# The ranking phase of a routed expert layer: statistics by chunk, tile products on ScalarE, reordered last steps, and logits with the gate stationary

## The chip, the cores and the metric

The kernel runs on one core of a Trainium2 chip. The metric is the device time of one execution in microseconds, as the median of several runs. The program computes a two-layer transformer with two expert layers; the change is in one phase near its end.

## What is computed

```python
x = x + attention(layernorm(x));  x = x + latent_moe(layernorm(x))
x = x + linear_attention(layernorm(x))
x = x + capacity_moe(layernorm(x))          # 4096 tokens of 256
# capacity_moe, up to the experts:
logits = x @ gate_weight.T                  # 128 experts, 48 of them kept
logits = where(old_to_new == -1, -inf, logits)
top_v, top_i = top_k(softmax(logits), 8)
top_v = top_v / sum(top_v)
oh = one_hot(old_to_new[top_i].reshape(-1)) # 4096*8 choices x 48 experts
pos = sum(cumsum(oh) * oh) - 1              # place of a choice in its expert's list
valid = pos < 96                            # an expert takes its first 96 tokens
# then each kept expert gathers its tokens, computes, and adds its weighted result back
```

## The kernel before, in words

Five engines run their own instruction lists, written out by hand, and wait for each other through semaphores. `ranking_phase` works on the 4096 tokens in 8 chunks of 512, each of four tiles of 128 tokens. It is a software pipeline of 13 steps: in step `i`, `now(i, back)` names chunk `i - back`, so different parts of the lists work on different chunks.

For a chunk, in order: VectorE finishes the residual sum of each tile (its first product, of `acc`, `rs` and `x`), takes its mean and variance (`variances`); ScalarE takes roots, VectorE `scales`, and ScalarE writes the normalized `lines`. TensorE transposes the lines into `tr` in PSUM. ScalarE copies them into a high part `XH` of reduced mantissa, VectorE subtracts that for the low part `XL`, and TensorE makes the logits `LG` from three products of high and low parts with the gate's `GH` and `GL`, with a penalty row `pen` for experts that are not kept. VectorE finds the top eight (`top`), the largest negated (`ntop`), and who was chosen (`left`, `sel`); ScalarE takes the exponentials `ex`. GpSimd sums choices (`tally`, `before`) and masks the exponentials (`es`). TensorE counts the places (`POS`), VectorE keeps those of the chosen (`u`), and GpSimd splits each into an eighth `hi` and a rest `lo` (`t2`, `hi`, `lo`). VectorE compares: `A` over `hi`, and `B`, eight compares over `lo`. Then B is multiplied by the token's number within its tile (`BB[0:8]`, the place products, ScalarE) and by the tile's first token (`BB[8:16]`, the tile products, GpSimd), and TensorE adds the products of A and BB into the slots `SL`. GpSimd also makes the weights `w`, which SP's queue stores to memory beside the lines.

The statistics are taken in four runs of two chunks (`RUNS`, `RT`, `RC`): run 0 and run 1 ahead of the loop, run 2 in step 1 and run 3 in step 3. Behind step 12, VectorE and TensorE turn the slots into the list `idx`. Then `kept_experts_phase` begins behind a barrier.

Of the kernel before, what the change touches and what calls it, by code (L numbers as in the profile page):

```python
# [25 lines left out]
P = 128  # L26
# [2110 lines left out]
def ranking_phase(nc, raw, o2n, x_rows, x_first, acc, rs, ident, rows, out, idx):  # L2137
# [12 lines left out]
    with Phase(nc, "rank") as ph:  # L2150
# [17 lines left out]
        absent = ph.sb("absent", [1, KEPT])  # L2168
        pen = ph.sb("pen", [1, 1, KEPT])
# [4 lines left out]
        tile_i = ph.sb("tile_i", [P, TILES, KEPT], I32)  # L2174
        tile_no = ph.sb("tile_no", [P, TILES, KEPT], BF16)
# [31 lines left out]
        POS = ph.ps("POS", [P, CHUNK])  # L2207
        SL = ph.ps("SL", [CAP, 2, CHUNK])
# [6 lines left out]
        (pe_lg, dve_top, dve_left, dve_ntop, dve_sel, act_ex, pool_es, dve_total, dve_share, pool_w, pool_tally,  # L2215
         pool_before, pe_pos, dve_u, pool_round, pool_hi, pool_lo, dve_a, dve_b, act_bp, pool_bt, pe_slots) = ph.sems(
            "pe_lg dve_top dve_left dve_ntop dve_sel act_ex pool_es dve_total dve_share pool_w pool_tally "
            "pool_before pe_pos dve_u pool_round pool_hi pool_lo dve_a dve_b act_bp pool_bt pe_slots")
# [3 lines left out]
        STEPS = CHUNKS + 5  # L2222

# [37 lines left out]
        def _(pool):  # L2261
# [3 lines left out]
            nc.gpsimd.iota(tile_i[:], [[P, TILES], [0, KEPT]], base=0, channel_multiplier=0).then_inc(iotas, 1)  # L2265
# [11 lines left out]
            for i in range(STEPS):  # L2277
                g = now(i, 2)
                if g is not None:

                    pool.wait_ge(dve_sel, g + 1)
                    nc.gpsimd.tensor_tensor(tally[:, 0], sel[:, g % 2, 0, :], sel[:, g % 2, 1, :], ALU.add)\
                        .then_inc(pool_tally, 1)
                    nc.gpsimd.tensor_tensor(tally[:, 1], sel[:, g % 2, 2, :], sel[:, g % 2, 3, :], ALU.add)\
                        .then_inc(pool_tally, 1)
                    pool.wait_ge(act_ex, g + 1)
                    if g >= 3:
                        pool.wait_ge(dve_total, g - 2)
                    nc.gpsimd.tensor_tensor(es[:, g % 3], ex[:, g % 2], sel[:, g % 2], ALU.mult).then_inc(pool_es, 1)
                    pool.wait_ge(pool_tally, 3 * g + 2)  # L2290
                    nc.gpsimd.tensor_tensor(tally[:, 2], tally[:, 0], tally[:, 1], ALU.add).then_inc(pool_tally, 1)
                    pool.wait_ge(pool_tally, 3 * g + 3)
                    if g >= 1:
                        pool.wait_ge(pool_before, g)
                        pool.wait_ge(pe_pos, g)
                    nc.gpsimd.tensor_tensor(before[:, (g + 1) % 2], before[:, g % 2], tally[:, 2], ALU.add)\
                        .then_inc(pool_before, 1)

                g = now(i, 4)
                if g is not None:  # L2300
                    pool.wait_ge(dve_share, g + 1)
                    nc.gpsimd.tensor_tensor(w[:, tiles_of(g), :], es[:, g % 3],
                                            total[:, g % 2].to_broadcast([P, TPC, KEPT]), ALU.mult).then_inc(pool_w, 1)
                    pool.wait_ge(dve_b, g + 1)
                    if g >= 3:
                        pool.wait_ge(pe_slots, g - 2)
# [4 lines left out]
                g = now(i, 2)  # L2311
# [14 lines left out]

        @block.tensor
        def _(pe):
# [7 lines left out]
            nc.tensor.matmul(tr[:, 1, KD * KEPT:(KD + 1) * KEPT], ones[:], perm[:], start=True, stop=True)\  # L2336
                .then_inc(pe_gp, 1)
            pe.wait_ge(gates_ready, 1)
            pe.wait_ge(pen_ready, 1)
            pe.wait_ge(slots_set, 1)  # L2340
            for i in range(STEPS):
# [11 lines left out]
                if g is not None:  # L2353

                    pe.wait_ge(low_ready, g + 1)
                    if g >= 2:
                        pe.wait_ge(dve_left, g - 1)
                        pe.wait_ge(act_ex, g - 1)
                    b = g % 2
# [45 lines left out]
        def _(act):  # L2405
# [23 lines left out]
            for i in range(STEPS):  # L2429
                if i + 1 < CHUNKS:  # L2430
                    make_lines(i + 1)
# [407 lines left out]
```

## Time and profile before

| | |
|---|---|
| median of 3 runs | 2995.62 us (2993.15 to 3000.16) |
| the profiled execution | 2990.76 us, its span 2988.4 us |
| ranking phase in the span | 2656.8 to 2798.2 us |
| expert phase behind it | 2799.1 to 2988.4 us |
| mean granted TensorE clock, whole span | 0.933 |
| busy share of the whole span | PE 91%, DVE 56%, ACT 47%, POOL 27% |

The names in the profile: PE is TensorE, PEld its weight loads, DVE VectorE, ACT ScalarE, POOL GpSimd and SP the engine whose queue issues the transfers here. Tiles of the phase have the prefix `rank_`. An instruction's row gives its start, its duration, its line, what it writes and reads, and in brackets the idle time of its engine ahead of it with what ended that. The shares are of the whole program, and the phase is a twentieth of it, so they tell nothing of the phase.

### The profile page before, as it was taken

Reading aid. Unit: us, or ns where it says so; the run is one execution under the profiler, and the core shown is the slowest. Engines: PE = TensorE matmul, PEld = TensorE weight load, DVE = VectorE, ACT = ScalarE, POOL = GpSimd, SP = SyncE. Lnnn points to the kernel's source line nnn. Section 1 sums busy time; section 2 is a strip of 40 time slices with the busy share of each in tenths; the row PEclk is TensorE's granted clock in tenths of the full one; section 3 lists DMA queues with packets and bytes.
Section 4 is the critical chain, followed back from the end, with each engine's and each line's share of the span. In section 5 each row is a group of like instructions: output and inputs, shape, how many; then the busy total and the mean of one; then the engine's idle time right before and its main releaser. Section 6 shows DMA issues by size and latency. Waiting matters only on the chain. (4 is left out here: it accounts for less than half of the span.)

```text
span 2988.4 us, 50873 instructions
## 1 busy us (share of the span) xinstructions
PE 2734.3 (91%) x17834; PEld 2218.9 (74%) x17834; DVE 1686.7 (56%) x3254; ACT 1394.1 (47%) x2564; POOL 815.0 (27%) x817
## 2 busy tenths in 40 slices
PE   7899999989799998699999999999999999978573
PEld 6444444368578887598998989899898999967452
DVE  7688888446588887544444444444444444456321
ACT  6477777756478876433333333333333333324110
POOL 3522121200152221122222222222222222215675
PEclk9799999989899999799999999999999999975665
DMA  8955464030254553200000000000000000022476
GB/s 254 202 94 80 67 87 60 3 97 4 97 203 179 188 182 131 81 1 8 16 1 22 1 23 1 1 22 1 22 1 22 1 1 19 1 85 78 104 171 123
DMA packets 158642, 204.15 MB, mean 68 GB/s; under 512 B 17568, under 2 KB 134976, under 8 KB 149696
## 3 DMA queue, kind: packets, MB, share of 16 engines
q1 hardware_dynamic: 149904, 186.14, 23.5%
q0 software_dynamic: 8544, 15.22, 3.0%
q8 instruction: 146, 2.39, 0.3%
q14 instruction: 48, 0.39, 0.0%
HBM read 154.74 MB, written 50.78 MB: 69 GB/s over the span
## 5 line engine op out<-in xcount | busy, mean ns | idle before, releaser
L1846 POOL TENSOR_TENSOR lin_o2sum<-lin_o2sum,lin_o 128x512 f32<-128x512 f32 x128 | 183.8, 1436 | 1020.7 <-ACT lin_o L1883 1020.7
L875 DVE TENSOR_REDUCE score_pm<-score_SM 128x1 f32<-128x512 f32 (+3 forms) x608 | 364.5, 656 | 80.6 <-PE score_SM L735 47.7
L829 ACT ACTIVATE score_PR<-score_SE 128x512 f32<-128x512 f32 (+1 forms) x640 | 309.8, 557 | 106.3 <-PE score_SE L763 102.7
L2101 DVE TENSOR_TENSOR C_acc<-lin_OUT,C_acc 128x512 f32<-128x512 f32 x256 | 177.2, 692 | 266.3 <-PE lin_OUT L1963 264.7
L2084 DVE SCALAR_TENSOR_TENSOR lin_go<-lin_gT,lin_O 128x512 f32<-128x512 f32 x128 | 88.1, 688 | 421.0 <-PE lin_O L1999 377.2
L1866 ACT ACTIVATE lin_qT<-lin_PJ 128x512 f32<-128x512 f32 x129 | 77.0, 597 | 434.3 <-PE lin_PJ L1925 434.3
L1925 PE MATMUL lin_PJ<-C_XH,lin_WH 128*128 128x512 f32 x774 | 254.4, 410 | 14.0 <-DVE lin_WL L2040 14.0
L1925 PE MATMUL lin_PJ<-C_XL,lin_WH 128*128 128x512 f32 x774 | 241.3, 393 | 0.0
L1925 PE MATMUL lin_PJ<-C_XH,lin_WL 128*128 128x512 f32 x774 | 241.1, 393 | 0.0
L735 PE MATMUL score_SM<-A_KR,A_QR 96*128 96x512 bf16 (+3 forms) x768 | 229.9, 341 | 12.1 <-DVEq L81 9.4
L763 PE MATMUL score_SE<-A_QR,A_KR 99*128 99x512 bf16 (+3 forms) x768 | 210.7, 330 | 2.0 <-ACT score_PR L829 1.5
L1888 ACT ACTIVATE lin_goh<-lin_go 128x512 fp32r<-128x512 f32 x128 | 81.0, 633 | 260.2 <-DVE lin_go L2084 260.2
L1636 ACT ACTIVATE experts_h<-experts_z 128x512 f32<-128x512 f32 x256 | 161.1, 629 | 70.5 <-DVE experts_z L1541 67.0
L1996 PE MATMUL lin_O<-lin_sd,lin_v 128*128 128x128 f32 x1024 | 190.4, 275 | 3.1 <-issue 3.1
L1541 DVE SCALAR_TENSOR_TENSOR experts_z<-experts_HP,experts_sq 128x512 f32<-128x512 f32 x256 | 174.0, 686 | 17.7 <-PE experts_HP L1673 14.3
L1841 POOL TENSOR_TENSOR lin_qd<-lin_qT,lin_dec 128x512 f32<-128x512 f32 x128 | 166.0, 1297 | 47.0 <-DVE lin_dec L2066 36.1
L1999 PE MATMUL lin_O<-lin_qd,lin_kv 128*128 128x128 f32 x896 | 173.5, 275 | 0.0
L1996 PEld LDWEIGHTS lin_O<-lin_sd,lin_v 128*128 128x128 f32 x1024 | 160.2, 191 | 14.3 <-issue 4.8
L702 POOL TENSOR_SCALAR_AFFINE_SELECT score_PR<-score_PR 128x512 f32<-128x512 f32 x128 | 79.7, 634 | 333.7 <-ACT score_PR L829 333.7
L1925 PEld LDWEIGHTS lin_PJ<-C_XL,lin_WH 128*128 128x128 f32 x774 | 145.9, 189 | 33.1
L1925 PEld LDWEIGHTS lin_PJ<-C_XH,lin_WL 128*128 128x128 f32 x774 | 145.7, 188 | 32.6
L1548 DVE TENSOR_TENSOR experts_hl<-experts_h,experts_hh 128x512 fp32r<-128x512 f32 x192 | 139.7, 727 | 33.0 <-ACT experts_hh L1637 24.4
(357 smaller groups left out, 6715.3 us busy)
## 6 DMA issues: line engine op xcount, KB each, us to landing
experts_sq<-B_roots SPq DMA_DIRECT2D x64, 1024.0 KB, 4.7
A_QR<-q_parts SPq DMA_DIRECT2D x96, 128.0 KB, 6.4
A_KR<-k_parts SPq DMA_DIRECT2D x96, 128.0 KB, 6.9
kept_GU<-L_ffn_gate_up_proj SPq DMA_DIRECT2D x48, 192.0 KB, 2.8
v_rows<-inp_vt SPq DMA_DIRECT2D x32, 256.0 KB, 4.0
A_V<-v_rows SPq DMA_DIRECT2D x16, 512.0 KB, 10.8
C_w<-L_attn_w_qkv SPq DMA_DIRECT2D x27, 256.0 KB, 3.6
q_parts<-inp_parts SPq DMA_DIRECT2D x16, 384.0 KB, 3.6
```

Of the source, the lines that this page charges most:

```text
L735: ins = nc.tensor.matmul(SM[:, count % RING, at:at + nk], QR[0:ROWS_QK, u, h0 + j, t * P:(t + 1) * P], KR[0:ROWS_QK, u, h0 + j, k0:k0 + nk ...
L763: ins = nc.tensor.matmul(SE[:, e % RING, at:at + nq], KR[0:ROWS_ALL, u, h, kt * P:(kt + 1) * P], QR[0:ROWS_ALL, u, h, q:q + nq], start=Tru ...
L829: nc.scalar.activation(PR[:, st % BUFS, h, 0:width], SE[:, e % RING, 0:width], ACT.Exp, scale=SCALE)\
L875: nc.vector.tensor_reduce(pm[:, n % 2, h0:h0 + nh, t, k0 // CHUNK], SM[:, count % RING, 0:nh * nk].rearrange("p (h k) -> p h k", h=nh), AX ...
L1541: nc.vector.scalar_tensor_tensor(z[:, e % 2], HP[:, e % BUFS], 0.0, sq[:, (e // QE) % BUFS, e % QE], ALU.max, ALU.mult).then_inc(dve_z, 1)
L1636: nc.scalar.activation(h[:, e % BUFS], z[:, e % 2], ACT.Square).then_inc(act_h, 1)
L1841: nc.gpsimd.tensor_tensor(qd[:], qT[:, j], dec[:, j, 0:1, :].to_broadcast([P, B4, BLK]), ALU.mult).then_inc(pool_qd, 1)
L1846: nc.gpsimd.tensor_tensor(o2sum[:, c], o2sum[:, c], o2[:], ALU.add).then_inc(pool_sum, 1)
L1925: ins = nc.tensor.matmul(PJ[:, bank], a[:, w, k, j * DH:(j + 1) * DH], x[:, k, :, c, :], start=(n == 0), stop=(n == 3 * KD - 1))
L1996: ins = nc.tensor.matmul(O[:, b, :], v[:, c % 2, b, j * DH:(j + 1) * DH], sd[:, b, :], start=True, stop=(c == 0))
L1999: ins = nc.tensor.matmul(O[:, b, :], kv[:, j, b, :], qd[:, b, :], start=False, stop=True)
L2101: nc.vector.tensor_tensor(dst, OUT[:, half], dst, ALU.add).then_inc(dve_acc[half], 1)
```

## The change

It has four parts.

1. *Statistics by chunk.* `variances(run)` over eight tiles becomes `statistics(g)` over four. Ahead of the loop stand chunk 0 and, behind the constants, chunk 1. The others stand at the ends of steps 0 to 4, as `STATS_AT` says. Roots and scales are taken for the ranges of chunks in `VARY`. ScalarE's lines of the next chunk now stand behind the high part and the new copy.
2. *Tile products on ScalarE.* GpSimd's product over 1536 columns becomes four ScalarE copies with a constant scale, one for each tile, over 8x48 columns. The table of tile numbers, its list and its cast go.
3. *Last steps.* From step 8 GpSimd rounds (`rounds`) ahead of making weights (`weights`). From step 9 VectorE makes `u` ahead of `A` and `B`.
4. *Logits.* The gate's columns become the stationary operand: six products over all 512 tokens into `LT`, 48 by 512. ScalarE copies it to `lt` and adds the penalty, now a column, as bias. Four transposes bring it back as `LG`.

```diff
+        VARY = [(0, 1), (1, 2), (2, 4), (4, 6), (6, 8)]
+        STATS_AT = {0: (2, 3), 1: (4,), 2: (5,), 3: (6,), 4: (7,)}
...
-                    nos = tile_no[:, tiles_of(g), :].rearrange("p (o t) e -> p o (t e)", o=1)
-                    nc.gpsimd.tensor_tensor(BB[:, g % 3, LO:2 * LO], B[:, g % 2], nos.to_broadcast([P, LO, COLS]),
-                                            ALU.mult).then_inc(pool_bt, 1)
+                if i < CHUNKS:
+                    weights(now(i, 4))
+                    rounds(now(i, 2))
+                else:
+                    rounds(now(i, 2))
+                    weights(now(i, 4))
         @block.tensor
-                    nc.tensor.matmul(LG[:, b, 0:COLS], ones[0:1, :], pen[:].to_broadcast([1, TPC, KEPT]),
-                                     start=True, stop=False, skip_group_check=True)
-                    for t in range(TPC):
-                        n = 0
-                        for x, W in ((XH, GH), (XL, GH), (XH, GL)):
-                            for k in range(KD):
-                                ins = nc.tensor.matmul(LG[:, b, t * KEPT:(t + 1) * KEPT], x[:, b, k, t * P:(t + 1) * P],
-                                                       W[:, k, :], start=False, stop=(n == 3 * KD - 1),
-                                                       skip_group_check=True)
-                                n += 1
+                    if g >= 1:
+                        pe.wait_ge(act_lt, g)
+                    n = 0
+                    for x, W in ((XH, GH), (XL, GH), (XH, GL)):
+                        for k in range(KD):
+                            ins = nc.tensor.matmul(LT[:], W[:, k, :], x[:, g % 2, k, :], start=(n == 0),
+                                                   stop=(n == 3 * KD - 1))
+                            n += 1
+                    ins.then_inc(pe_lt, 1)
...
+                g = now(i, 1)
+                    pe.wait_ge(act_lt, g + 1)
+                    for t in range(TPC):
+                        ins = nc.tensor.transpose(LG[:, g % 2, t * KEPT:(t + 1) * KEPT], lt[:, t * P:(t + 1) * P],
+                                                  ident[0:KEPT, 0:KEPT])
...
+                for run in run_of(i + 1):
+                    roots(run)
...
+                    act.wait_ge(pe_lt, g + 1)
+                    nc.scalar.activation(lt[:], LT[:], ACT.Identity, bias=pen[:, 0:1]).then_inc(act_lt, 1)
+                if i + 1 < CHUNKS:
+                    make_lines(i + 1)
...
+                    for j in range(TPC):
+                        part = slice(j * KEPT, (j + 1) * KEPT)
+                        ins = nc.scalar.activation(BB[:, g % 3, LO:2 * LO, part], B[:, g % 2, :, part], ACT.Copy,
+                                                   scale=float((g * TPC + j) * P))
...
+                if i >= CHUNKS + 1:
+                    place_in_list(now(i, 2))
...
+                for g in STATS_AT.get(i, ()):
+                    statistics(g)
```

On ScalarE, one step in the middle of the loop, first of before and then of the change; the names are those of the tiles above.

```order
L2422 ACTIVATE rank_lines<-rank_x_rest,rank_shift,rank_rstd 128x256 x4
L2437 ACTIVATE rank_XH<-rank_tr 128x1024
L2445 ACTIVATE rank_BB<-rank_B,rank_place 128x1536
L2455 ACTIVATE rank_ex<-rank_LG,rank_ntop 128x48 x4
L2415 ACT_TABLE_LOAD
L2415 ACTIVATE rank_std<-rank_std 128x8
```

```order
L2451 ACTIVATE rank_XH<-rank_tr 128x1024
L2458 ACTIVATE rank_lt<-rank_LT,rank_pen 48x512
L2435 ACTIVATE rank_lines<-rank_x_rest,rank_shift,rank_rstd 128x256 x4
L2468 ACTIVATE rank_BB<-rank_B,rank_place 128x1536
L2472 ACTIVATE rank_BB<-rank_B 128x8x48 x4
L2483 ACTIVATE rank_ex<-rank_LG,rank_ntop 128x48 x4
```

The high part moved ahead of the lines, and five operations joined: the copy of the logits and four tile products.

On VectorE, the start of the phase up to the first low part of the loop; the rows are those of the change, and before had eight tiles (x8) in each of the two groups of three.

```order
L2497 SCALAR_TENSOR_TENSOR D_x_first<-C_acc,C_rs,D_x_first 128x256 x4
L2501 BN_STATS rank_stats<-D_x_first 128x6 x4
L2504 BN_AGGR rank_mv<-rank_stats 128x2 x4
...
L2542 TENSOR_SCALAR rank_perm<-rank_cols,rank_known 128x48
L2497 SCALAR_TENSOR_TENSOR D_x_first<-C_acc,C_rs,D_x_first 128x256 x4
L2501 BN_STATS rank_stats<-D_x_first 128x6 x4
L2504 BN_AGGR rank_mv<-rank_stats 128x2 x4
...
L2546 TENSOR_TENSOR rank_GL<-rank_tr,rank_GH 128x96
...
L2557 TENSOR_TENSOR rank_XL<-rank_tr,rank_XH 128x1024
```

Half of the statistics moved from ahead of the gate's low part GL to behind it.

On VectorE, the last two steps with compares (chunks 6 and 7), first of before and then of the change.

```order
L2532 TENSOR_TENSOR rank_A<-rank_hi,rank_step_no 128x2304
L2538 TENSOR_SCALAR rank_B<-rank_lo 128x192 x8
L2544 TENSOR_REDUCE rank_total<-rank_es 128x4
L2554 RECIPROCAL rank_total<-rank_total 128x4
L2570 TENSOR_TENSOR rank_u<-rank_POS,rank_sel 128x192
L2532 TENSOR_TENSOR rank_A<-rank_hi,rank_step_no 128x2304
L2538 TENSOR_SCALAR rank_B<-rank_lo 128x192 x8
```

```order
L2524 TENSOR_TENSOR rank_u<-rank_POS,rank_sel 128x192
L2567 TENSOR_TENSOR rank_A<-rank_hi,rank_step_no 128x2304
L2573 TENSOR_SCALAR rank_B<-rank_lo 128x192 x8
L2579 TENSOR_REDUCE rank_total<-rank_es 128x4
L2589 RECIPROCAL rank_total<-rank_total 128x4
L2567 TENSOR_TENSOR rank_A<-rank_hi,rank_step_no 128x2304
L2573 TENSOR_SCALAR rank_B<-rank_lo 128x192 x8
```

The product u of chunk 7 moved from behind the compares of chunk 6 to ahead of them.

## Rows read from the trace of the kernel before

**Rows 1.** Windows: start:end, length, busy of each engine, granted clock, DMA share, GB/s
```profile
2674.50:2749.30 74.80, 65.98 (x344) 59.73 (x345) 48.05 (x198) 37.28 (x68) 29.46 (x49) 0.52 0.28 92
2749.30:2798.20 48.90, 23.82 (x175) 22.03 (x173) 33.03 (x83) 8.03 (x13) 32.23 (x32) 0.53 0.05 11
2799.10:2988.40 189.30, 112.45 (x576) 83.44 (x576) 40.76 (x150) 24.45 (x97) 123.22 (x106) 0.64 0.73 155
```

**Rows 2.** Timeline ahead of the loop: start, us, engine line op, tiles, count [idle before]
```profile
2657.94 3.19 DVE L2469 SCALAR_TENSOR_TENSOR D_x_first<-C_acc,C_rs,D_x_first 128x256 f32<-128x256 f32 x8
2663.79 0.64 DVE L2476 BATCH_NORM_AGGREGATE rank_mv<-rank_stats 128x2 f32<-128x6 f32 x8
2665.52 0.95 DVE L2497 CAST rank_tile_no<-rank_tile_i 128x1536 bf16<-128x1536 int32 x1
2674.50 1.94 PE L2349 MATMUL rank_tr<-ident,rank_lines 128*128 128x128 f32 x8 [5.61 <-DVE rank_GL L2509]
```

**Rows 3.** Timeline of the loop, VectorE and ScalarE
```profile
2677.53 1.23 DVE L2524 TENSOR_TENSOR rank_XL<-rank_tr,rank_XH 128x1024 fp32r<-128x1024 f32 x1 [3.13 <-ACT rank_XH L2437]
2706.54 1.22 DVE L2524 TENSOR_TENSOR rank_XL<-rank_tr,rank_XH 128x1024 fp32r<-128x1024 f32 x1
2711.81 0.25 DVE L2579 TENSOR_SCALAR rank_sel<-rank_left 128x192 bf16<-128x192 f32 x1
2724.12 1.28 ACT L2415 ACT_TABLE_LOAD   x1
2726.09 2.07 ACT L2422 ACTIVATE rank_lines<-rank_x_rest,rank_shift,rank_rstd 128x256 f32<-128x256 f32 x4 [0.47 <-DVE rank_shift L2486]
2728.07 1.00 ACT L2437 ACTIVATE rank_XH<-rank_tr 128x1024 fp32r<-128x1024 f32 x1
2748.08 1.22 DVE L2524 TENSOR_TENSOR rank_XL<-rank_tr,rank_XH 128x1024 fp32r<-128x1024 f32 x1 [1.47 <-ACT rank_XH L2437]
```

**Rows 4.** Timeline of VectorE and GpSimd, a step of the loop and one of the tail
```profile
2720.46 1.03 DVE L2538 TENSOR_SCALAR rank_B<-rank_lo 128x192 bf16<-128x192 bf16 x8
2759.70 1.41 DVE L2532 TENSOR_TENSOR rank_A<-rank_hi,rank_step_no 128x2304 bf16<-128x2304 bf16 x1 [2.22 <-POOL rank_lo L2325]
2761.03 4.98 DVE L2538 TENSOR_SCALAR rank_B<-rank_lo 128x192 bf16<-128x192 bf16 x8
2762.75 3.08 POOL L2308 TENSOR_TENSOR rank_BB<-rank_B,rank_tile_no 128x1536 bf16<-128x1536 bf16 x1
```

**Rows 5.** Groups by line and form in the phase: busy us, mean ns | idle before
```profile
L2538 DVE TENSOR_SCALAR rank_B<-rank_lo 128x192 bf16<-128x192 bf16 x64 | 22.5, 421 | 0.0
```

**Rows 6.** Timeline of the last steps, VectorE and GpSimd
```profile
2777.03 0.34 DVE L2570 TENSOR_TENSOR rank_u<-rank_POS,rank_sel 128x192 f32<-128x192 f32 x1
2786.26 3.08 POOL L2308 TENSOR_TENSOR rank_BB<-rank_B,rank_tile_no 128x1536 bf16<-128x1536 bf16 x1
2797.91 0.20 DVE L2600 TENSOR_TENSOR D_idx<-rank_tok,rank_unused 96x48 uint32<-96x48 f32 x1
```

**Rows 7.** Timeline of ScalarE: a 256-column copy, the exponentials, the place products
```profile
2657.56 0.38 ACT L2407 ACTIVATE rank_GT<-rank_tr 128x256 f32<-128x256 f32 x1 [2.05 <-PE rank_tr L2330]
2723.23 0.87 ACT L2455 ACTIVATE rank_ex<-rank_LG,rank_ntop 128x48 f32<-128x48 f32 x4 [5.04 <-DVE rank_ntop L2558]
2728.97 1.56 ACT L2445 ACTIVATE rank_BB<-rank_B,rank_place 128x1536 bf16<-128x1536 bf16 x1
```

**Rows 8.** Timeline of TensorE: logits in a step, and 512 columns elsewhere
```profile
2720.00 1.00 PE L2360 MATMUL rank_LG<-rank_pen,rank_ones 1*128 1x192 f32 x2
2726.08 0.36 PE L2380 MATMUL rank_POS<-rank_before,rank_eighths 128*128 128x192 bf16 x1
807.47 0.63 PE L1671 MATMUL experts_HP<-B_LH,B_W1H 128*128 128x512 f32 x1
```

**Rows 9.** Windows, as in group 1, around the last row of group 8
```profile
805.00:809.00 4.00, 4.00 (x10) 3.13 (x11) 2.12 (x3) 0.00 (x0) 0.00 (x0) 0.50 1.04 339
```

**Rows 10.** Timeline of VectorE, eight first products of the statistics beside GpSimd's work
```profile
2699.49 3.64 DVE L2469 SCALAR_TENSOR_TENSOR rank_x_rest<-C_acc,C_rs,rank_x_rest 128x256 f32<-128x256 f32 x8
```

More of the change, by code:

```diff
@@ L2222, in ranking_phase, with run_of @@
         STEPS = CHUNKS + 5
+        VARY = [(0, 1), (1, 2), (2, 4), (4, 6), (6, 8)]
+        STATS_AT = {0: (2, 3), 1: (4,), 2: (5,), 3: (6,), 4: (7,)}
+        def run_of(g):
+            return [r for r, (first, _) in enumerate(VARY) if first == g]
         def now(i, back):
@@ L2275, in _, with weights @@
             pool.wait_ge(fixed, 1)
[L2277 to L2299, printed above, removed]
+            def weights(g):
                 if g is not None:
@@ L2325, in _ @@
                     nc.gpsimd.tensor_tensor(lo[:, g % 2], u[:, g % 2], hi[:, g % 2], ALU.subtract).then_inc(pool_lo, 1)
+            for i in range(STEPS):
+                g = now(i, 2)
+                if g is not None:
+                    pool.wait_ge(dve_sel, g + 1)
+                    nc.gpsimd.tensor_tensor(tally[:, 0], sel[:, g % 2, 0, :], sel[:, g % 2, 1, :], ALU.add)\
+                        .then_inc(pool_tally, 1)
+                    nc.gpsimd.tensor_tensor(tally[:, 1], sel[:, g % 2, 2, :], sel[:, g % 2, 3, :], ALU.add)\
+                        .then_inc(pool_tally, 1)
+                    pool.wait_ge(act_ex, g + 1)
+                    if g >= 3:
+                        pool.wait_ge(dve_total, g - 2)
+                        pool.wait_ge(pool_w, g - 2)
+                    nc.gpsimd.tensor_tensor(es[:, g % 3], ex[:, g % 2], sel[:, g % 2], ALU.mult).then_inc(pool_es, 1)
+                    pool.wait_ge(pool_tally, 3 * g + 2)
+                    nc.gpsimd.tensor_tensor(tally[:, 2], tally[:, 0], tally[:, 1], ALU.add).then_inc(pool_tally, 1)
+                    pool.wait_ge(pool_tally, 3 * g + 3)
+                    if g >= 1:
+                        pool.wait_ge(pool_before, g)
+                        pool.wait_ge(pe_pos, g)
+                    nc.gpsimd.tensor_tensor(before[:, (g + 1) % 2], before[:, g % 2], tally[:, 2], ALU.add)\
+                        .then_inc(pool_before, 1)
+                if i < CHUNKS:
[4 more added lines that the diff above has]
+                    weights(now(i, 4))
         @block.tensor
@@ L2461, in _, with statistics @@
             tt, ts = nc.vector.tensor_tensor, nc.vector.tensor_scalar
-            def variances(run):
-                tiles = range(run * RT, (run + 1) * RT)
-                if run:
-                    dve.wait_ge(x_in[run - 1], 16)
+            def statistics(g):
+                tiles = range(g * TPC, (g + 1) * TPC)
+                if g >= RC and g % RC == 0:
+                    dve.wait_ge(x_in[g // RC - 1], 16)
                 for t in tiles:
@@ L2487, in scales, with place_in_list @@
                                                ALU.mult, ALU.mult).then_inc(scale_ready, 1)
+            def place_in_list(g):
+                if g is not None:
+                    dve.wait_ge(pe_pos, g + 1)
+                    if g >= 2:
+                        dve.wait_ge(pool_lo, g - 1)
+                    tt(u[:, g % 2], POS[:, 0:COLS], sel[:, g % 2].rearrange("p t e -> p (t e)"), ALU.mult)\
+                        .then_inc(dve_u, 1)
             nc.vector.memset(SL[:], 0.0).then_inc(slots_set, 1)
-            variances(0)
+            statistics(0)
             scales(0)
-            dve.wait_ge(iotas, 5)
+            dve.wait_ge(iotas, 4)
             nc.vector.tensor_copy(cols[:], cols_i[:]).then_inc(dve_unused, 1)
@@ L2505, in _ @@
             ts(perm[:], cols[:], known[:, 0:1], None, ALU.is_equal).then_inc(fixed, 1)
-            variances(1)
+            statistics(1)
             dve.wait_ge(pe_gp, 1)
@@ L2564, in _ @@
                     ins.then_inc(dve_left, 1)
[L2565 to L2571 removed]
+                if i < CHUNKS + 1:
+                    place_in_list(now(i, 2))
                 g = now(i, 1)
```

95 lines of the change are left out of this document (44 added, 51 removed).

## The prediction

> **What bounds it now.** Only the ranking phase changes, so I read its stretch of the trace and leave out the 2657 us ahead of it. The windows come first, then the timeline around the chunk-by-chunk markers. The loop (first transposes to the last low part) and the tail (to the list of places) show no engine that is busy throughout: TensorE has 66.0 of 74.8 us and VectorE 48.1 in the loop, and in the tail no engine passes 33.0 of 48.9 [rows 1]. TensorE looks like the bound of the loop, but it runs at a mean granted clock of 0.52, almost all of it at the lower of its two levels (1.2 GHz), and what ends VectorE's wait for a chunk is ScalarE's high part [rows 3]. So the phase is a chain from engine to engine, and I follow its markers. Ahead of the loop TensorE idles 5.61 us until VectorE has written GL at 2674.5; there VectorE is behind with statistics [rows 2]. The low parts of chunks 0 and 7 start at 2677.53 and 2748.08, which is 70.55 us for seven steps [rows 3]. The phase's last write starts at 2797.91, so the tail behind the last low part is 50 us [rows 3, 6].
>
> **The head.** VectorE handles 16 tiles of statistics before GL, 8 on each side of the constants; now it handles 4 and 4. From the first product to the end of the aggregates, 8 tiles take 2657.94 to 2664.43, so 0.81 us a tile [rows 2]; eight tiles fewer save 6.5. The cast of tile numbers, 0.95, falls away too [rows 2]. TensorE is waiting for exactly this, so the head is worth **7.5 us**. GpSimd's list of tile numbers goes too, but VectorE does not wait for it.
>
> **The loop.** A chunk's statistics now stand in steps 0 to 4 (two chunks in step 0), 3.25 us each. One whole pass of VectorE, low part to chosen experts without a wait, takes 2706.54 to 2712.06, or 5.5 us [rows 3]. The first steps have no A (1.4) and no B (1.0) in it [rows 4], nor the row sums, so there it is about 3.1. ScalarE's high part takes 1.0, a table load 1.28 [rows 3]. Its lines (2.07) stood between the exponentials and the high part, and now stand behind the high part, off this path. From low part to low part:
> - 0 to 1: low part 1.1, two chunks of statistics 6.5, root and scale 0.5, high part 1.0: 9.1.
> - 1 to 2: 3.1 and 3.25, with 0.2 for the logits: 6.5.
> - 2 to 3: 6.4, a wait of 1.2 for the logits, table load and root 1.5, high part 1.0: 10.1.
> - 3 to 4: 5.5 and 3.25: 8.8.
> - 4 to 5: 8.8, table load and root 1.5, high part 1.0, handing over 0.2: 11.5.
> - 5 to 6: no statistics are left, and ScalarE is the longer one: copy of the logits 0.6, lines 2.0, place products 1.5, tile products 1.8, table load 1.3, exponentials 0.9, high part 1.0: 9.1 [rows 3, 7].
> - 6 to 7: the same without a table load, 7.8.
>
> The sum is 62.9 against 70.55. I subtract 0.9 for collisions of the statistics with GpSimd (below) and take **7 us**.
>
> Three prices in it have no row of their own. *Tile products*: four ScalarE operations of 8x48 columns. The nearest are a copy of 256 columns at 0.38 and of 1024 at 1.00 [rows 3, 7]; on that line 384 columns take 0.46 and, overlapping, four take 1.8. Below, they cannot cost less than one operation over all 1536 columns, 1.56 [rows 7]; above, four times the 1024-column copy, 4.0. *Copy of the logits*, 512 columns: 0.6 on the same line. *Logits*: six products of 512 columns. The profile has such a product at 0.63 us from start to end, ten starting in 4.0 us at clock 0.50 [rows 8, 9], hence 0.4 each and 2.6 for six; the old ones, with their penalty row, took 2720.00 to 2726.08, 6.1 us [rows 8]. At the upper level of the clock six would take 1.3, with weight loads in between 3.8. Neither end matters much: with the transposes in (2.0), the transposes back (four of 48 columns, at most half of these, 0.9), the positions (0.5) and the slot products (2.8), TensorE needs 8.8 a step, no more than VectorE or ScalarE. So 3.5 us a step come off TensorE, and most of them are not on the path; the copy and the transposes back take back 1.5 of them in any case.
>
> **The tail.** Here most of the gain lies. B, eight compares, takes 1.03 us in a step of the loop and 4.98 in the tail; it ends when GpSimd's tile products (2762.75 to 2765.83) end [rows 4]. All eight B together take 22.5 us [rows 5], and at 1.03 each they would take 8.2: 14.3 us are lost, all in the last four steps (4 x 1.03 and 18.4), and there VectorE's next row sums, maxima, and positions queue behind B, and GpSimd behind them. With the tile products on ScalarE, GpSimd still has sums and weights of 0.3 to 0.5 us each beside B; the first 1.7 of the 4.98 were spent beside these [rows 4]. I leave 0.8 in each of the four and take 11. If those small ones keep each B at 3.0, the gain is 6.4; if nothing is left, 14.3.
>
> The Trainium skill (SBUF — State Buffer, "Who interferes with whom") says that VectorE in a two-port mode, or with two SBUF inputs, shares an exclusive port with GpSimd, and that the second to issue waits for the whole of the other's instruction. The B rows agree. By it alone the small GpSimd operations would hold up B too, which is my lower value of 6.4.
>
> The moved products u of chunk 7 are started before A and B of chunk 6 instead of behind them (u was at 2777.03 [rows 6]). Behind u stands GpSimd's rounding; with B short, VectorE would reach u about when GpSimd is through its own sums, so I give it 0.5 only. At the very end GpSimd's last tile products (3.08, from 2786.26, a microsecond behind B [rows 6]) become place and tile products in a row on ScalarE, 1.5 and 1.8: 0.7 shorter. Together 12.2; I take off 0.7 for ScalarE, which now does 3.3 for each chunk while the steps shorten: **11.5 us**. GpSimd's weights of a chunk are now later than its rounding, and only a store hangs on them, which ends ahead of the list.
>
> **The rest.** The experts behind it, 189.3 us, get the same inputs. GpSimd is busy in 123.2 of it and DMA moves 155 GB/s; the DMA share in the tail is 0.05, so nothing of the ranking runs into it [rows 1]. I count nothing there. SP's queue keeps its order.
>
> **Sum.** 7.5 + 7 + 11.5 = 26 us. The profiled execution took 2990.8, 2.4 more than its span of 2988.4, so it would take 2964.8. The median of the runs, 2995.6, is 4.9 above it: **2970 us**, 0.9% faster. A change of 0.2% or 6 us is about what can be told from none.
>
> **The rivals.**
> - *The statistics collide with GpSimd.* The first product of each tile has two SBUF inputs; in steps 1 to 4 it now starts just when GpSimd starts rounding. By row, eight of them beside GpSimd took 3.64 against 3.19 alone [rows 2, 10], 0.45 for two chunks, from which I took 0.9 for four. If each waits for the whole of GpSimd's instruction, up to 1.6 is lost in each of four steps: gain 20, 2976 us. Chance 0.10. It is what the Trainium skill's rule above (SBUF — State Buffer, "Who interferes with whom") would give for two SBUF inputs; the row shows much less.
> - *ScalarE becomes the bound of all later steps.* With tile products at 4.0 a chunk, 2.2 more lie on the path in the last two steps of the loop, at the last chunk, and partly in two steps of the tail: about 9 us, gain 17, 2979 us. For it: ScalarE gets 3.0 a step more when it also loads tables. Against it: the line through two rows. Chance 0.12.
> - *It ends slower.* If the strided reading made each tile product cost as much as the whole 1536-column operation, 1.6 us, a chunk would need 6.3. ScalarE would then take 12.3 or more from step 4 on, where 8 to 9 are there: 4.5 in each of two steps and 17 over the tail, which eats the 26. From 1.7 us each on it is slower. No row has so dear a column. Chance 0.02; near no change, 2993, 0.04.
> - *More than forecast.* B quite undisturbed and TensorE's clock at its upper level in the loop give 32: 2964 us. Chance 0.04.
>
> **How the numbers follow.** The forecast (gain 20 to 31) has 0.68. From 2962 to 2982, a gain of 14 to 34, the range takes in the first two rivals in most of their width and the bounds of B (6.4 to 14.3) and of the tile products; what is left out, dearer tile products and more, is under 0.2. Faster by over 0.2%: 0.68 + 0.10 + 0.12 + 0.04 = 0.94; same 0.04; slower 0.02.
>
> **What would show it.** TensorE's first transposes should start some 7.5 us sooner, ended by GL still. From the first to the last low part 62 to 65 us. B at most 2 us in the tail; no GpSimd instruction near 3 us. Tile products at 0.4 to 0.5 each. The forecast is wrong if B stays near 5 us without the tile products, if low parts wait for VectorE's statistics by more than 3.5 us a chunk, or if the experts' stretch leaves 189 us by more than 3.

## The result and the profile after

The changed kernel takes **2960.9 us** (median of 4 runs, 2959.6 to 2965.65) against 2995.55 us before: ratio 0.9885, 95% interval 0.9868 to 0.9903, 34.65 us faster. The forecast was 2970 with a range from 2962. The direction was right, the size too small: the range ends 1.1 us above the median. The forecast put 26 us on the phase, and the phase gives 32.9 (table below). The profiled execution took 2959.6 us, its span 2957.0.

Windows of the profile after, the stretches that answer to [rows 1] (start:end, length, busy of each engine, granted clock, DMA share, GB/s), and one step of the loop:

```profile
2665.50:2729.50 64.00, 38.53 (x213) 27.23 (x213) 53.11 (x228) 47.58 (x92) 21.44 (x46) 0.71 0.43 141
2729.50:2764.10 34.60, 18.36 (x177) 15.63 (x176) 21.20 (x84) 17.43 (x34) 16.86 (x27) 0.75 0.07 15
2765.10:2956.90 191.80, 114.40 (x576) 88.02 (x576) 36.63 (x150) 24.43 (x97) 123.20 (x106) 0.62 0.71 153
2721.00:2728.30 7.30, 4.88 (x47) 3.57 (x47) 5.53 (x27) 7.30 (x16) 2.59 (x6) 1.00 0.50 158
```

The loop with its first transposes and last low part takes 64.0 us instead of 74.8, the stretch to the list 34.6 instead of 48.9. TensorE falls from 66.0 busy us to 38.5 in the loop, and the clock granted to it rises from 0.52 to 0.71. The experts take 191.8 us, 2.5 more than in [rows 1]; e14 says what that is.

Timeline of the head and the loop after (start, duration, engine, line, tiles, in brackets the idle time ahead and what ended it); it answers to [rows 2, 3, 8]:

```profile
2665.39 0.26 DVE L2546 TENSOR_TENSOR rank_GL<-rank_tr,rank_GH 128x96 fp32r<-128x96 f32 x1
...
2665.80 1.94 PE L2357 MATMUL rank_tr<-ident,rank_lines 128*128 128x128 f32 x8 [2.38 <-DVE rank_GL L2546]
...
2668.84 1.23 DVE L2557 TENSOR_TENSOR rank_XL<-rank_tr,rank_XH 128x1024 fp32r<-128x1024 f32 x1 [2.67 <-ACT rank_XH L2451]
...
2685.94 0.56 DVE L2584 MAX8 rank_top<-rank_LG 128x8 f32<-128x48 f32 x4 [0.36 <-PE rank_LG L2397]
...
2688.41 1.28 ACT L2425 ACT_TABLE_LOAD   x1
...
2691.46 0.18 DVE L2509 TENSOR_SCALAR rank_std<-rank_mv 128x8 f32<-128x8 f32 x1
...
2691.67 0.21 ACT L2425 ACTIVATE rank_std<-rank_std 128x8 f32<-128x8 f32 x1 [1.98 <-DVE rank_std L2509]
...
2707.25 1.19 POOL L2294 TENSOR_SCALAR rank_t<-rank_u 128x192 f32<-128x192 f32 x1 [4.35 <-DVE rank_u L2524]
...
2728.30 1.22 DVE L2557 TENSOR_TENSOR rank_XL<-rank_tr,rank_XH 128x1024 fp32r<-128x1024 f32 x1 [1.76 <-ACT rank_XH L2451]
```

The first transposes are still ended by GL, which comes at 2665.39 instead of 2673.83. The low parts of chunks 0 and 7 start 59.46 us apart, not 70.55. The maxima of chunk 1 wait only 0.36 us for their logits. The table load for the root stands at 2688.41, well ahead of the variance at 2691.46 that the root waits for.

Timeline of the tail after, answering to [rows 4, 6]:

```profile
2736.72 1.41 DVE L2567 TENSOR_TENSOR rank_A<-rank_hi,rank_step_no 128x2304 bf16<-128x2304 bf16 x1 [2.22 <-POOL rank_lo L2303]
...
2736.87 1.39 POOL L2312 TENSOR_TENSOR rank_tally<-rank_sel 128x48 bf16<-128x48 bf16 x1
...
2738.05 1.72 DVE L2573 TENSOR_SCALAR rank_B<-rank_lo 128x192 bf16<-128x192 bf16 x8
...
2742.62 0.36 DVE L2524 TENSOR_TENSOR rank_u<-rank_POS,rank_sel 128x192 f32<-128x192 f32 x1 [0.76 <-PE rank_POS L2387]
...
2749.64 1.65 DVE L2567 TENSOR_TENSOR rank_A<-rank_hi,rank_step_no 128x2304 bf16<-128x2304 bf16 x1 [1.68 <-POOL rank_lo L2303]
...
2754.07 1.74 ACT L2472 ACTIVATE rank_BB<-rank_B 128x384 bf16<-128x384 bf16 x4
...
2755.96 2.77 PE L2408 MATMUL rank_SL<-rank_BB,rank_A 128*96 128x128 bf16 x24 [3.55 <-ACT rank_BB L2472]
...
2763.83 0.20 DVE L2632 TENSOR_TENSOR D_idx<-rank_tok,rank_unused 96x48 uint32<-96x48 f32 x1
```

B is 1.72 where it was 4.98, and the last u comes 14.3 us behind the last low part, where it was 29.0. Groups by line of the phase after (busy us, mean ns of one | idle before), tile products and B, to [rows 5]:

```profile
L2472 ACT ACTIVATE rank_BB<-rank_B 128x384 bf16<-128x384 bf16 x32 | 14.1, 524 | 0.0
...
L2573 DVE TENSOR_SCALAR rank_B<-rank_lo 128x192 bf16<-128x192 bf16 x64 | 10.6, 238 | 0.0
```

The four tile products of a chunk cost 1.74 to 1.79 us, 0.52 each, and B 10.6 us in all instead of 22.5.

Because the code around the phase does not change, I measure the phase by itself in every run: *head* from the start of VectorE's clearing of SL to the first low part, *loop* to the last low part, *tail* to the start of the last write of the list, all three by the starts of rows in the trace. The ratio is against runs of the kernel before on the same chip, whose medians lie between 2993.4 and 2995.0 us in the experiments, so medians of different rows tell less than the ratios and the phase. Two executions, one of e8 and one of e9, took 6376 and 8295 us and are left out here.

| kernel | head | loop | tail | phase | median us | ratio to before (95%) |
|---|---|---|---|---|---|---|
| before | 20.42 | 70.55 | 49.83 | 140.80 | 2995.55 | 1 |
| after | 12.95 | 59.46 | 35.53 | 107.94 | 2960.90 | 0.9885 (0.9868 to 0.9903) |
| e1 tile products back | 13.80 | 65.83 | 49.18 | 128.81 | 2983.02 | 0.9961 (0.9947 to 0.9975) |
| e2 statistics back | 19.57 | 60.96 | 36.08 | 116.61 | 2968.98 | 0.9918 (0.9902 to 0.9935) |
| e3 logits back | 13.21 | 61.14 | 36.35 | 110.70 | 2962.88 | 0.9896 (0.9880 to 0.9913) |
| e4 last steps back | 12.96 | 59.92 | 37.08 | 109.96 | 2964.71 | 0.9898 (0.9881 to 0.9914) |
| e5 lines first | 13.33 | 70.91 | 36.37 | 120.61 | 2972.98 | 0.9932 (0.9915 to 0.9948) |
| e6 products alone | 19.55 | 67.80 | 37.06 | 124.41 | 2977.69 | 0.9944 (0.9927 to 0.9961) |
| e8 statistics alone | 14.24 | 74.19 | 49.69 | 138.12 | 2993.55 | 1.0000 (0.9990 to 1.0010) |
| e16 lines alone | 20.43 | 71.09 | 49.86 | 141.38 | 2995.35 | 1.0003 (0.9993 to 1.0013) |
| e9 tail order | 12.95 | 60.01 | 32.66 | 105.62 | 2959.31 | 0.9883 (0.9863 to 0.9903) |
| e10 root waits twice | 12.96 | 62.03 | 34.37 | 109.36 | 2965.22, one run | |
| e11 table early | 12.96 | 59.91 | 35.26 | 108.13 | 2963.18 | 0.9896 (0.9879 to 0.9912) |
| e12 tail and table | 12.96 | 59.85 | 32.47 | 105.28 | 2956.38 | 0.9875 (0.9859 to 0.9892) |
| e13 changed again | 12.97 | 59.54 | 35.56 | 108.07 | 2961.41 | 0.9898 (0.9881 to 0.9915) |
| e14 before again | 20.42 | 70.57 | 48.71 | 139.70 | 2992.04, one run | |
| e15 before once more | 20.42 | 70.54 | 49.83 | 140.79 | 2995.29, one run | |

### The profile page after: what moved, and what is told of

The parts are those of the page before. It is cut to its first block and busy times, and to the rows that moved or that the text cites. A ratio compares the mean times of both kernels' runs of the same rounds, so it can differ in the third digit from the quotient of the medians.

```text
span 2957.0 us, 50661 instructions
## 1 busy us (share of the span) xinstructions
PE 2703.8 (91%) x17706; PEld 2184.6 (74%) x17706; DVE 1668.0 (56%) x3256; ACT 1411.9 (48%) x2605; POOL 789.5 (27%) x808
## 5 line engine op out<-in xcount | busy, mean ns | idle before, releaser
L1541 DVE SCALAR_TENSOR_TENSOR experts_z<-experts_HP,experts_sq 128x512 f32<-128x512 f32 x256 | 174.2, 686 | 17.5 <-PE experts_HP L1673 14.3
L1548 DVE TENSOR_TENSOR experts_hl<-experts_h,experts_hh 128x512 fp32r<-128x512 f32 x192 | 139.5, 727 | 32.9 <-ACT experts_hh L1637 23.6
## 6 DMA issues: line engine op xcount, KB each, us to landing
kept_GU<-L_ffn_gate_up_proj SPq DMA_DIRECT2D x48, 192.0 KB
```

The source lines that it names most:

```text
L1541: nc.vector.scalar_tensor_tensor(z[:, e % 2], HP[:, e % BUFS], 0.0, sq[:, (e // QE) % BUFS, e % QE], ALU.max, ALU.mult).then_inc(dve_z, 1)
```

## The experiments

**Undoing one part at a time.** e1 puts the tile products back on GpSimd, with their table of tile numbers:

```diff
-                    for j in range(TPC):
-                        ins = nc.scalar.activation(BB[:, g % 3, LO:2 * LO, part], B[:, g % 2, :, part], ACT.Copy, ...)
+                    nc.gpsimd.tensor_tensor(BB[:, g % 3, LO:2 * LO], B[:, g % 2], nos.to_broadcast([P, LO, COLS]), ...)
```

> The changed kernel with its second part undone: the tile products are again one GpSimd product of 128x1536 with a table of tile numbers (its cast, 0.95 us, is back ahead of the loop). Theory: the tail gained its 14 us because B no longer stands beside GpSimd's 3.08 us product. Then B in the last four steps goes back to 4 to 5 us each, the stretch from the last low part to the list goes from 35.5 to 46 to 49 us, the loop stays within 2 us of 59.5, and the time is about 2975 us (2972 to 2979). Rival: the tail gained by the new order of its last steps and by shorter logits; then B is still slow, but the tail stays under 41 us and the time under 2968 us.

The phase gets 20.9 us longer. Of this 13.7 lie in the tail, which ends 0.2 above the expected range, but 6.4 in the loop, against the 2 that the theory allowed, and the time lies above its range. Only two of the last four B go back to 4 us or more (4.51 and 4.18); the other two take 1.73 and 1.76. Timeline of e1 in the tail:

```profile
2743.12 4.51 DVE L2578 TENSOR_SCALAR rank_B<-rank_lo 128x192 bf16<-128x192 bf16 x8
...
2744.11 3.10 POOL L2295 TENSOR_TENSOR rank_BB<-rank_B,rank_tile_no 128x1536 bf16<-128x1536 bf16 x1
...
2759.70 4.20 POOL L2295 TENSOR_TENSOR rank_BB<-rank_B,rank_tile_no 128x1536 bf16<-128x1536 bf16 x1
...
2764.00 1.76 DVE L2578 TENSOR_SCALAR rank_B<-rank_lo 128x192 bf16<-128x192 bf16 x8 [3.04 <-POOL rank_BB L2295]
```

The first pair is a B that runs beside the product and ends 0.4 us behind it. The last pair is the same cost in another form: the product takes 4.20 us, and a later B waits 3.04 us for its end, since it needs the buffer that the product reads. GpSimd's long product delays B either way.

e2 takes the statistics in runs of two chunks again, four chunks ahead of the loop and the others at the start of steps 1 and 3:

```diff
-        VARY = [(0, 1), (1, 2), (2, 4), (4, 6), (6, 8)]
-        STATS_AT = {0: (2, 3), 1: (4,), 2: (5,), 3: (6,), 4: (7,)}
+        VARY = [(0, 2), (2, 4), (4, 6), (6, 8)]
+        STATS_AT = {1: (4, 5), 3: (6, 7)}
```

> The changed kernel with the statistics again in four runs of two chunks (two runs ahead of the loop, one each at the start of steps 1 and 3), the lines still behind the high part. Theory A, from the prediction's sum: the head is worth its 6.5 us, and what the loop takes on is hidden or nearly so; undone, the first low part comes at about 2675.3 us and the loop gets shorter by 2 us at most, so the time is 2965 to 2968 us. Theory B: VectorE is the bound of the loop's first five steps, so that the eight tiles only move; the first low part 6.5 us later, the loop shorter by 5 to 7, and the time within 2 us of 2961.

Theory A is right on the head, which is 6.6 longer, and theory B falls: the loop does not shrink at all but grows by 1.5, although it has two chunks less of statistics. A had it shrink by up to 2, and the time is 1 us above A's range.

e3 takes back the logits by tokens, with their penalty row:

```diff
-                            ins = nc.tensor.matmul(LT[:], W[:, k, :], x[:, g % 2, k, :], ...)
+                                ins = nc.tensor.matmul(LG[:, b, t * KEPT:(t + 1) * KEPT], x[:, b, k, t * P:(t + 1) * P], W[:, k, :], ...)
```

> The changed kernel with its fourth part undone: logits in 24 short products and a penalty row, no copy of the logits and no transposes back. Theory: off the path as predicted, the old logits cost or give 2 us at most (time 2959 to 2963 us, loop 58 to 61 us). Rival: with the other parts in place TensorE is the bound of the loop, since it was busy 62.8 us of 70.55 before; then the loop goes to 64 to 68 us, the tail gets some 2 us longer, and the time is 2967 to 2972 us.

The rival falls: TensorE is busy 55.9 of the loop's 61.1 us, and the loop is only 1.7 longer. The theory stands at the edge, 0.1 outside for the loop. One step carries it, 2 to 3, with 10.87 us instead of 8.44. Its row:

```profile
2687.56 0.56 DVE L2570 MAX8 rank_top<-rank_LG 128x8 f32<-128x48 f32 x4 [2.80 <-PE rank_LG L2372]
```

There the maxima wait 2.80 us for logits, where the changed kernel waits 0.36.

e4 puts the last steps back in their old order:

```diff
-                if i >= CHUNKS + 1:
-                    place_in_list(now(i, 2))
...
-                if i < CHUNKS + 1:
+                if i < STEPS:
                     place_in_list(now(i, 2))
```

> The changed kernel with its third part undone: in the last steps weights ahead of rounding on GpSimd, A and B ahead of u on VectorE. Theory, from the prediction's sum: it is worth 0.5 to 1 us, so the last u stands some 3 us later but its rounding waits for GpSimd's own sums anyway; tail 36 to 37.5 us, time 2961 to 2963 us. Rival: it is worth 3 us or more, the length of A and B (1.65 and 1.84), since rounding of the last chunk is the chain that ends last; tail 38.5 us or more, time 2964 us or more.

The tail, 37.08, lies in the theory's range and the time in the rival's: 1.55 us of tail and 2.0 of phase. The tail alone is three times what the prediction gave it; the other 0.46 lies in the loop, which the edit does not touch (see the scatter below).

e5 puts the lines back ahead of the high part, a move to which the change's description gives one sentence:

```diff
                 for run in run_of(i + 1):
                     roots(run)
+                if i + 1 < CHUNKS:
+                    make_lines(i + 1)
```

> The changed kernel with ScalarE's lines of the next chunk back ahead of the high part. Theory: moved lines gave about 2 us (their length is 2.07) in those of the seven loop steps in which VectorE waits for the high part behind a root or behind the exponentials, four or more of them; undone, the loop goes from 59.5 to 66 to 69 us, the ranking phase from 107.9 to 115 to 118 us. Rival: while VectorE takes statistics ScalarE idles, and the lines are written there wherever they stand; the loop stays under 62.5 us.

The theory was right in kind and short in size: the loop is 11.45 us longer and as long as before the change. Timeline of one step of e5:

```profile
2719.03 0.21 ACT L2425 ACTIVATE rank_std<-rank_std 128x8 f32<-128x8 f32 x1 [1.96 <-DVE rank_std L2509]
...
2719.84 2.07 ACT L2435 ACTIVATE rank_lines<-rank_x_rest,rank_shift,rank_rstd 128x256 f32<-128x256 f32 x4 [0.60 <-DVE rank_shift L2516]
...
2721.82 1.00 ACT L2453 ACTIVATE rank_XH<-rank_tr 128x1024 fp32r<-128x1024 f32 x1
...
2722.85 1.22 DVE L2557 TENSOR_TENSOR rank_XL<-rank_tr,rank_XH 128x1024 fp32r<-128x1024 f32 x1 [3.05 <-ACT rank_XH L2453]
```

The lines stand between root and high part, and VectorE waits 3.05 us for that high part (0.39 at the same chunk of the changed kernel).

**Doing one part alone.** e6, e8 and e16 put the tile products on ScalarE, the statistics by chunk, and the lines behind the high part into the kernel before, each by itself with the edits shown above.

> The kernel before with the second part alone: tile products on ScalarE. Theory: it gives what undoing it took away, B of 1.3 to 2.1 us in the tail, the tail 49.8 to 36 to 39 us, the loop 66 to 70 us, the ranking phase 140.8 to 121 to 126 us. Rival: without the moved lines and the shorter logits ScalarE (lines, high part, exponentials and now 3.3 us of products) sets the loop; it gets no shorter or longer (70 to 76 us), and the phase is 127 to 135 us. In this kernel the length of the experts' stretch also tells whether the 193 to 195 us seen with the change (190.5 before) belong to one of its other parts.

As the theory had it: tail 12.8 shorter, loop 2.75 shorter, phase 124.4.

> The kernel before with the statistics by chunk alone, the lines still ahead of the high part. Theory: undoing this part in the changed kernel made the phase 8.7 us longer, all but 2 of it ahead of the loop; here TensorE and GpSimd are the slower ones in the loop, so the statistics hide in it as well or better: head 20.4 to 13, loop 69 to 72 us, the phase 140.8 to 132 to 135 us. Rival: the root's wait now stands in a step that the statistics lengthen and the lines are late for it; the loop takes back the head's gain (74 us or more), and the phase is 138 us or more.

The theory falls and the rival holds: the head gives 6.2 us and the loop takes back 3.6; phase 138.1, 2.7 better, and no change that the median can tell. The lines, late behind each root as in e5, make VectorE wait 3.05 us for the high part of chunks 0, 1, 3 and 5.

> The kernel before with ScalarE's lines of the next chunk behind the high part and its root still ahead, and nothing else. Theory: this reordering was the largest term of the loop, which the prediction named but gave no sum of its own; alone it takes 2 us from most of the seven steps until TensorE, busy 62.8 of 70.55 us, is the bound: loop 62 to 66 us, phase 131 to 137 us. Rival: GpSimd's tile products and the old logits hold the chain in those steps, and it only counts together with the other parts: loop 68 us or more.

The rival holds: nothing is gained. Groups of the phase in e16, B and GpSimd's tile products:

```profile
L2544 DVE TENSOR_SCALAR rank_B<-rank_lo 128x192 bf16<-128x192 bf16 x64 | 31.2, 557 | 0.0
...
L2308 POOL TENSOR_TENSOR rank_BB<-rank_B,rank_tile_no 128x1536 bf16<-128x1536 bf16 x8 | 29.2, 3651 | 0.0
```

B takes 31.2 us instead of 22.5 [rows 5]: in three steps of the loop it now stands beside GpSimd's product and takes 3.9 us, where it came behind that product before and took 1.03. A, which met the product before, takes 12.0 us in all instead of 14.7. So the two together cost 6.0 us more, and the loop ends 0.5 longer. That this collision is what eats the gain is read from the rows; a kernel with the lines and the tile products moved together, without the rest, was not run.

**The table load.** e10 gives the root a second wait, on what is always ready ahead of the first:

```diff
                 act.wait_ge(var_ready, run + 1)
+                act.wait_ge(mv_ready, VARY[run][1] * TPC)
```

> The changed kernel with a second wait ahead of each root, on the aggregates, which always end before the variance that it waits for already. Theory: a table load stands between an instruction's waits where it has several; with one it goes ahead of the wait and costs nothing, which is why the steps behind a root were 8.4 and 10.45 us where the prediction, with the load on the path, had 10.1 and 11.5. With two waits the load of 1.28 us comes behind the first one, and the steps 2 to 3 and 4 to 5 of the loop get 1.2 to 1.3 us longer each, the loop 59.5 to 61.9 to 62.2 us. Rival: the load comes early in any case, or VectorE's other work covers it; the loop stays within 0.6 us.

Timeline of e10, the wait for chunk 1's logits, the variance, the load and the root:

```profile
2690.17 0.56 DVE L2585 MAX8 rank_top<-rank_LG 128x8 f32<-128x48 f32 x4 [0.82 <-PE rank_LG L2397]
...
2695.52 0.42 DVE L2510 TENSOR_SCALAR rank_std<-rank_mv 128x8 f32<-128x8 f32 x1
...
2695.56 1.28 ACT L2426 ACT_TABLE_LOAD   x1 [2.94 <-DVE rank_mv L2505]
...
2696.86 0.21 ACT L2426 ACTIVATE rank_std<-rank_std 128x8 f32<-128x8 f32 x1
```

The load now comes behind the aggregates, and the steps 2 to 3 and 4 to 5 take 9.85 and 11.57 us: 1.41 and 1.12 more. Of the 1.41, 0.46 is a longer wait for chunk 1's logits (0.82 instead of 0.36), so an exposed load is worth 1.0 to 1.1 us here. The loop, 62.03, is within a microsecond of the 62.9 that the prediction added up, and every step within 0.5. The phase is only 1.4 longer, because the last slot products ran faster this time (1.51 instead of 2.77 us; see the scatter below). The Trainium skill (ScalarE: Activation LUTs, "What ACT_TABLE_LOAD costs") gives 1283 ns for a load and some 1380 more for a drain; the trace agrees with the first (1.28). In e10 the root follows the load by 0.02 us, and in the changed kernel the load at 2688.41 follows the exponentials by 0.02, so the second does not show here.

e11 loads the exponentials' table behind the lines of steps 1, 3 and 5:

```diff
                     make_lines(i + 1)
+                if i in (1, 3, 5):
+                    act.preload_act_table(ACT.Exp)
```

> The changed kernel with the table of the exponentials loaded by an instruction of its own behind the lines of steps 1, 3 and 5, ahead of the waits for the choices. Theory: the load in step 3 (behind 2.67 us of waiting now) hides, but VectorE's statistics set that step and ScalarE has no gap in step 5, so the loop gets shorter by 0.3 to 1.5 us and the phase is 106.5 to 107.6 us. Rival: the exponentials' loads are on the path in both steps, and the loop gets 2.5 us shorter or more.

Missed: the phase is 108.13, no better. Timeline of e11 in the step that should have gained:

```profile
2701.53 1.28 ACT L2462 ACT_TABLE_LOAD   x1
...
2704.19 0.88 ACT L2485 ACTIVATE rank_ex<-rank_LG,rank_ntop 128x48 f32<-128x48 f32 x4 [1.38 <-DVE rank_ntop L2595]
...
2708.01 1.19 DVE L2559 TENSOR_TENSOR rank_XL<-rank_tr,rank_XH 128x1024 fp32r<-128x1024 f32 x1
```

The load did move into a gap, and the exponentials come 1.28 sooner; but the next low part waits for nothing on ScalarE, its statistics end just ahead of it.

**More of the same.** e9 finds chunk 7's choices ahead of A and B of chunk 5, drops GpSimd's last sums, and rounds chunk 7 ahead of masking it. e12 adds e11's load.

> The changed kernel with more of its last steps reordered: in step 8 VectorE finds the choices of chunk 7 and makes u of chunk 6 ahead of A and B of chunk 5, and GpSimd drops the sums of the last chunk that nothing reads and rounds that chunk ahead of masking it. Theory: the tail is a chain through rounding on GpSimd, A and B, and not a load on any engine; the last A, at 2749.6 before, starts 3 to 5 us sooner, tail 35.5 to 30.5 to 32.5 us, phase 103 to 105 us. Rival: A and B of chunk 5 come later by as much (1.8 us of choices, 2 of waiting), the products of chunks 5 and 6 on ScalarE then stand in the way of those of chunk 7, and the tail stays at 34 us or more.

> The last steps reordered as in e9 and the table loaded early as in e11, together. Theory: tail 32.7 us and loop as in e11, so the ranking phase is 104 to 105.5 us and the time 0.1% below that of the changed kernel (2 to 4 us), at the edge of what can be measured. Rival: one of the two only moves a wait, and the phase stays at 107 us or more.

The tail is 2.9 us shorter in e9, just short of what was expected, and 3.1 in e12. Timeline of e12, last A and list:

```profile
2745.09 1.69 DVE L2540 TENSOR_TENSOR rank_A<-rank_hi,rank_step_no 128x2304 bf16<-128x2304 bf16 x1 [0.39 <-POOL rank_lo L2303]
...
2760.22 0.20 DVE L2647 TENSOR_TENSOR D_idx<-rank_tok,rank_unused 96x48 uint32<-96x48 f32 x1
```

The last A starts 17.3 us behind the last low part (21.3 after). Against e13, the changed kernel on the same chip, e12's median is 5.0 us lower (2954.96 to 2957.95, against 2959.96 to 2967.93): the fastest kernel of the study, though the two intervals of the ratios overlap, and the phase accounts for 2.8 of the 5.0.

**The scatter.**

> The changed kernel once more, for the scatter of what it doesn't touch. Theory: the ranking phase takes 107.9 us within 0.5, while the stretch ahead of it (2655.9) and the experts behind (193.2) move by 2 to 5 us from run to run in kernels that are alike there; so the median shows a gain of 32 to 36 us that the phase shows as 32.9. Rival: the 2.7 us by which the experts were longer than before belong to the change, and are seen again at 193 us or more with the same start.

> The kernel before once more, for the scatter of what the change doesn't touch. Theory: the stretch ahead of the ranking phase and the experts behind it scatter by some us whatever the kernel; the ranking phase is 140.8 us within 0.5, and the experts, 190.5 before, lie among the 192 to 195 us of the other kernels. Rival: a shorter experts' stretch belongs to the kernel before, 191 us or less again, and the change pays 2 to 4 us there.

> As e14, the same kernel a second time, so that one odd execution does not decide: theory, experts 192 to 195 us in one of the two at least; rival, 191 us or less in both.

The phase of the changed kernel comes again within 0.13 us, but other runs show that it can move by more. e4 and e9 change nothing ahead of step 8, and yet their loops are 0.46 and 0.55 longer. It lies in the step from 2 to 3, where the maxima wait for chunk 1's logits. Timeline and window of e4 there, and the window of the changed kernel:

```profile
2689.99 0.56 DVE L2584 MAX8 rank_top<-rank_LG 128x8 f32<-128x48 f32 x4 [1.01 <-PE rank_LG L2397]
...
2687.80:2690.00 2.20, 1.97 (x12) 0.93 (x10) 1.19 (x4) 1.25 (x3) 0.00 (x0) 0.60 0.16 51
2684.40:2686.00 1.60, 1.04 (x11) 0.63 (x9) 1.24 (x4) 1.28 (x3) 0.00 (x0) 1.00 0.11 35
```

TensorE's clock was granted at 1.00 in that stretch of the changed kernel and at 0.60 in e4, the last two products for the logits took 1.06 us instead of 0.63, and the wait was 1.01 us instead of 0.36. So a difference of some 0.6 us in the loop is within what the same code does.

Behind the list, the kernel before takes 193.2 us in both repeats, like all the others (192.0 to 194.7), so its first profile with 190.5 was the odd one and the change pays nothing there. e14's phase is 1.1 short of the expected 140.8. Timeline of the last slot products, in the first profile of before and in e14:

```profile
2789.49 2.77 PE L2395 MATMUL rank_SL<-rank_BB,rank_A 128*96 128x128 bf16 x24 [2.23 <-POOL rank_BB L2308]
...
2789.39 1.63 PE L2395 MATMUL rank_SL<-rank_BB,rank_A 128*96 128x128 bf16 x24 [2.23 <-POOL rank_BB L2308]
```

The clock granted in the stretch of these products was 0.50 in the first (2789.0 to 2792.2) and 0.89 in e14 (2789.0 to 2791.1): a good microsecond of the phase's end is the clock of that moment. In the changed kernel and in all other runs but e10 they took 2.76 or 2.77.

## Why the prediction fell short

- **Head, 7.5 us.** Measured 7.47 (20.42 to 12.95). Each term was right: the tiles' 6.5 (6.6 in e2) and the cast (0.87 in e6).
- **Loop, 7 us.** Measured 11.1. The step that failed is "2 to 3: ... a wait of 1.2 for the logits, table load and root 1.5" and its like, 4 to 5, which put the load on the path. These were given 10.1 and 11.5 us and took 8.44 and 10.45, 2.7 together; the others lie within 0.2, but for the last two, 0.35 and 0.5 shorter than their sums. The load ahead of a root, an instruction with one wait, ran while ScalarE waited (2688.41 against the variance at 2691.46). e10 forces it behind a wait and gets the prediction's size. The other part is the logits: the maxima waited 0.36 us (up to 1.01 in other runs), not 1.2, and 2.80 with the old logits in e3. The rows of before could not tell: the variance there was long done when its load began at 2724.12 [rows 3], so ScalarE had nothing to wait for. Timeline of before, that variance:

```profile
2706.46 0.17 DVE L2479 TENSOR_SCALAR rank_std<-rank_mv 128x8 f32<-128x8 f32 x1
```

- **The collisions, 0.9.** Their size was about right: four first products of the statistics beside GpSimd's rounding took 1.91 or 1.92 us against 1.64 alone, in three steps. But no step was over its sum by more than 0.2, so the 0.9 taken off the gain came on top of steps that had been given too much time already. The rival with whole instructions did not come: GpSimd's rounding beside them took 1.19 instead of 0.86, not more.
- **Tail, 11.5 us.** Measured 14.3, the second term that was too small. B in the last four steps fell from 18.4 to 6.5, or 11.9 us, against 11. The moved u was given 0.5 and is worth 1.5 (e4); the 0.7 taken off for ScalarE did not show, since it waits for B in the last steps.
- **The tile products, 0.4 to 0.5.** Nearly right: 0.52 each (the line through the two rows of [rows 3, 7] gives 0.48 for 384 columns, not the 0.46 of the prediction), and ScalarE is the bound of the last two loop steps (7.30 of 7.30 us) at the 8.8 and 7.3 us forecast as 9.1 and 7.8. The two rivals that rested on dear products are out.
- **The moved lines.** They were a clause, "off this path", and no term. e5 makes them worth 11.5 us of loop, e16 nothing alone. The prediction came near by adding whole steps, which holds such an interaction; parts priced one by one would not have: the five undone cost some 47 us together (20.9, 12.7, 8.7, 2.8, 2.0) where the change gives 32.9.
- **The median.** I added the 4.9 us by which before's median stood above its profile. It was 1.3 for the changed kernel. The phase explains 32.9 of the 34.65, and the rest is within the scatter of what does not change: in the runs the phase starts at 2653.7 to 2661.6 us, and what is behind it takes 190.5 to 194.7.

Nearest to the result was the last rival, 2964, but not by its reasons. B is not undisturbed (1.3 to 1.8 us in the last four steps, not 1.03), and the clock of the loop is 0.73 and not the upper level; with the old logits (e3) it is 0.58, and the loop only 1.7 us longer.

## What to carry to other kernels

In a chain from engine to engine, add up whole steps with the new order, and expect the parts to work only together: shortening one link moves its neighbour onto the next collision. A long GpSimd operation over two SBUF tensors beside VectorE's compares costs both engines (B 4.98 instead of 1.03 us, the product up to 4.20 instead of 3.08); ScalarE's rows showed no such stretch (place products 1.57 to 1.60 us throughout the changed kernel). Look where the program puts a table load against the waits of its instruction before putting it on the path.

## What the hardware showed that was not expected

TensorE's clock was higher where TensorE had less to do. In the loop of before it was busy 62.8 of 70.55 us at a granted clock of 0.52; in the changed kernel 36.0 of 59.46 at 0.73, and in the step shown above 4.88 of 7.30 at 1.00, the upper level. What differs is the kind of work: six products of 512 columns in place of 24 of 48. With the old logits in the changed kernel (e3) the clock was 0.58 at 55.9 busy us of 61.1. A smaller busy share alone does not go with a higher clock: in e5, with the new logits too, TensorE was busy 37.2 of 70.91 us at 0.66. Why, no run here tells.

A takes GpSimd with it: a sum of choices that takes 0.27 us alone took 1.39 beside A and ended 0.13 behind it. The Trainium skill (SBUF — State Buffer, "Who interferes with whom") has it that a VectorE instruction with two SBUF inputs contends with a GpSimd instruction that reads SBUF, over ports that it calls an exclusive lock. Here the trace agrees: the sum does not get through before A ends. For B's eight short compares beside GpSimd's short operations the cost was small, 1.3 to 1.8 us instead of 1.03.
